# First pass of a decoder layer: the softplus of the state-space block summed by VectorE instead of by identity products in PSUM

## The chip, the core and the metric

The kernel runs on one core of one Trainium2 chip. The metric is the device time of one execution in microseconds (us). Times of single instructions below are in nanoseconds (ns) or us, as marked.

## What is computed

One decoder layer over 128 sequences of 128 positions and width 256. It has three parts, each with a residual and a layer norm: a selective state-space block (Mamba), a cross attention with FiLM and a long convolution, and a mixture FFN. The change touches only the first one, and there only the step size `dt`:

```
xz = einsum('bld,ed->ble', x, in_proj_w);  xc, z = split(xz)
xs = silu(conv1d(xc) + conv_b)
dt, B, C = split(einsum('bld,rd->blr', xs, x_proj_w), [64, 80])
dt = softplus(einsum('blr,dr->bld', dt, dt_proj_w) + dt_proj_b)      # 512 channels
...
h[t] = exp(dt*A) * h[t-1] + dt*B*xs;   y[t] = sum over 16 states of h[t]*C[t]
```

With v the argument of the softplus, e = exp(-|v|) and w = -(1+e) rounded, the kernel computes softplus(v) as relu(v) + ln(-w) + r, where r = e + (w + 1) is what the rounding of w lost. So each element of `dt` is a sum of three terms.

## The kernel before, in words

The program has a setup and three passes over the data, with a barrier of all engines between them. Pass 1 (`pass1`) holds the state-space block, the first half of the cross attention (scores, top-k, softmax, FiLM) and ends at about 5.1 ms of the profile. It works on 32 blocks of 4 sequences (512 columns). The 512 channels are 4 chunks `c` of 128 partitions; each chunk has 16 states; so a block has 64 **units** `u`, one scan each.

For one unit: ScalarE makes the decay exp(dt*A) (`decay`, L1049). VectorE scans (`tensor_tensor_scan`, L1180 for odd units, L1184 for even ones). GpSimd multiplies the scanned state by C four units later (`times_c`, L1255), and TensorE adds it up over the states by an identity product in PSUM (`sum_states`, L877). The input of the scan is dt*B*xs: for even units GpSimd makes it (L1268), for odd units ScalarE scales the transposed product (L1036) and TensorE transposes it (L862). The scanned states lie in a ring of 8 tiles, so GpSimd's L1268 of unit u waits for TensorE's sum of unit u-8.

There is no scheduler. Every engine runs its own list in order, and all meet by semaphores (`need`). While block i is scanned, the steps of the **front** of block i+1 and of the **back** of block i-1 are put between the units by hand: the tables `PE_AT`, `ACT_AT`, `DVE_AT` and `POOL_AT` say after which unit a step is issued on each engine. The steps that matter here:

- `dt0` to `dt3` (ScalarE, after units 31 to 38): |v| into `small` (L952) and relu(v) into `dt` (L954).
- `se` (ScalarE, 39): e = exp(-|v|) in `small` (L959), then w into `uu` (L962).
- `sr` (VectorE, 38): r into `small` (L1111), over all four chunks at once.
- `sl` (ScalarE, 40): ln(-w) in `uu` (L965), with a load of the table of Ln before it and one of Exp behind it.
- `ds0` to `ds3`: TensorE (42, 43, 44, 51) adds r, ln and relu of one chunk in PSUM by three products with the identity (L775, L777, L779), and ScalarE (44, 46, 48, 52) copies the sum into `dt` (L968).
- `sp0` to `sp3` (GpSimd, 45, 48, 53, 59): dt*xs (L1247), which waits for `dt` of its chunk. GpSimd's products of later units are queued behind it.
- `tka` to `tkd` and `sm` with a number (VectorE): top-k and softmax of the back of the block before; each `tk` is four MAX8 and four MATCH_REPLACE8 (L1137, L1141), `sm` is L1152 and L1158. `sc2`, `sc3` (L824, L825) and `at2` (L833) are score and attention products on TensorE, and `sm2` on ScalarE (L995) is the exponential that VectorE's `sm2` waits for.

`PER` has the counts of the semaphores for one block, and `BANK` gives the tiles of the steps two PSUM banks in turn.

Of the kernel before, what the change touches and what calls it, by code (L numbers as in the profile page):

```python
# [78 lines left out]
    ld_C0=128, ld_C1=128, ld_C2=128, ld_C3=128, bt_mm=1, bt=1, ut_mm=4, ut=4,  # L79
    vabs=4, vrelu=4, vexp=1, w1=1, rest=1, vln=1, ds_mm=4, dt=4, u=4,  # L80
    decay=64, bx=32, bxt=32, bxp=32, scan=64, hc=64, nsum=64, y=4, yg=4,
# [12 lines left out]
PE_AT = dict(xc0=2, xc1=3, xc2=6, xc3=7, op0=8, op1=8, op2=9, op3=10, z0=13, z1=13, z2=14, x1T=17, z3=19, qk=21,  # L94
             sc0=22, xp=24, bt=26, dt0=29, sc1=29, dt1=30, dt2=34, at0=35, dt3=36, sc2=36, at1=40, ds0=42, ds1=43,
             ds2=44, sc3=45, at2=49, ds3=51, tu0=53, at3=53, xa=54, tu1=55, film0=56, film1=58, tu2=59, film2=60,
             tu3=60, film3=62)
ACT_AT = dict(xc0=5, y3=5, xc1=5, xc2=6, xc3=9, z0=12, x1=14, z1=14, z2=15, x1T=16, z3=19, qk=23, si=24, xp=26,
              sm0=26, bt=28, dt0=31, dg0=31, dt1=33, dt2=34, sm1=36, dt3=38, at0=39, se=39, dg1=39, sl=40, at1=42,
              sm2=44, ds0=44, ds1=46, dg2=46, ds2=48, at2=49, sm3=50, ds3=52, dg3=52, at3=53, tu0=53, xa=54, tu1=56,  # L100
              tu2=62, tu3=63)
DVE_AT = dict(xc0=4, xc1=4, xc2=5, xc3=6, ln1=12, ln2=18, tka0=24, tkb0=24, tkc0=24, tkd0=26, sm0=26, tka1=31,
              tkb1=32, tkc1=33, tkd1=34, sm1=35, tka2=38, sr=38, tkb2=39, tkc2=40, tkd2=41, sm2=42, tka3=46, tkb3=47,
              tkc3=48, tkd3=49, sm3=49, film0=57, film1=59, film2=62, film3=63)
# [3 lines left out]
def steps_at(table, u, which):  # L108
# [8 lines left out]
    dt0=("vrelu", 1), dt1=("vrelu", 2), dt2=("vrelu", 3), dt3=("vrelu", 4),  # L117
    ds0=("dt", 1), ds1=("dt", 2), ds2=("dt", 3), ds3=("dt", 4),
    tu0=("ut", 1), tu1=("ut", 2), tu2=("ut", 3), tu3=("ut", 4),
# [369 lines left out]
def pass1(nc, sems, i_, arena, psum, x1_d, xa_d, xin_d, wf_d, bc_d, kr_d, sh, NB):  # L489
    with ExitStack() as ctx:  # L490
# [72 lines left out]
        def tile_ps(name):  # L563
            return side[:, BANK[name]]
# [148 lines left out]
        def _(pe):  # L713
# [14 lines left out]
            def step(name, i, par, other, which):  # L728
# [33 lines left out]
                elif name[:2] == "tu":  # L762
# [6 lines left out]
                    mm.then_inc(S["ut_mm"], 1)  # L769
                elif name[:2] == "ds":  # L770

                    c = int(name[-1])
                    ps = bank(name)
                    need(pe, "rest", i, 1)
                    pe.matmul(ps, ident, small[:, c], start=True, stop=False)  # L775
                    need(pe, "vln", i, 1)
                    pe.matmul(ps, ident, uu[par][:, c], start=False, stop=False)  # L777
                    need(pe, "vrelu", i, c + 1)
                    pe.matmul(ps, ident, dt[par][:, c], start=False, stop=True).then_inc(S["ds_mm"], 1)  # L779
                elif name[:2] == "op":  # L780
# [133 lines left out]
        def _(act):  # L914
            def step(name, i, par):
# [29 lines left out]
                elif name[:2] == "dt":  # L945
                    need(act, "dt_mm", i, c + 1)
                    if c == 0:
                        need(act, "ds_mm", i - 1, C)
                        need(act, "st_xin", i - 3, 64)
                        need(act, "q_mm", i - 2, 1)  # L950
                        need(act, "u", i - 2, C)
# [11 lines left out]
                elif name == "sl":  # L963
                    need(act, "rest", i, 1)
                    act.activation(uu[par], uu[par], ACT.Ln, scale=-1.0).then_inc(S["vln"], 1)  # L965
                elif name[:2] == "ds":
                    need(act, "ds_mm", i, c + 1)
                    act.copy(dt[par][:, c], tile_ps(name)).then_inc(S["dt"], 1)  # L968
                elif name == "x1":
# [117 lines left out]
        def _(dve):  # L1087
# [8 lines left out]
            def step(name, i, par):  # L1096
# [11 lines left out]
                elif name == "sr":  # L1108

                    need(dve, "w1", i, 1)  # L1110
                    dve.scalar_tensor_tensor(out=small, in0=uu[par], scalar=1.0, in1=small, op0=ALU.add, op1=ALU.add)\  # L1111
                       .then_inc(S["rest"], 1)
                elif name == "ln1":
                    need(dve, "ld_x", i, 16)
# [56 lines left out]
            def iteration(i, par, front, back):  # L1171
                names = which_steps(front, back)
                for u in range(C * NS):
                    need(dve, "decay", i, u + 1)
                    s = ring[:, u % RING]
                    if through_pe(u):
                        need(dve, "bxp", i, u // 2 + 1)
                        j, w = before(i, u, RING)
                        need(dve, "nsum", j, w + 1)
                        dve.tensor_tensor_scan(s, decay_sb[:, u // 2 % 2], bx_ps[:, u // 2 % 2], 0.0, ALU.mult, ALU.add)\  # L1180
                            .then_inc(S["scan"], 1)
                    else:
                        need(dve, "bx", i, u // 2 + 1)
                        dve.tensor_tensor_scan(s, decay_ps[:, u // 2 % 2], s, 0.0, ALU.mult, ALU.add)\  # L1184
                            .then_inc(S["scan"], 1)
                    for st in steps_at(DVE_AT, u, names):
                        if st == "film0" and front:
                            need(dve, "ds_mm", i + 1, C)
                        if st in FRONT:
                            step(st, i + 1, 1 - par)  # L1190
                        else:
                            step(st, i - 1, 1 - par)
# [748 lines left out]
```

## Time and profile before

| | |
|---|---|
| median of 3 runs | 7288.89 us (7283.7 to 7292.69) |
| the profiled execution | 7288.94 us, its span 7287.1 us |
| granted clock of TensorE, mean | 0.955 |
| busy share of the span: TensorE, VectorE, ScalarE, GpSimd | 92%, 74%, 61%, 63% |

The profile is of one execution. An instruction's row has its start, its length, its engine, its line in the program, its tiles (`arena` is all of SBUF, `psum` all of PSUM), and in brackets how long the engine sat idle before it and what ended the wait. Matmuls are pipelined: a row of two or four products of 512 columns is longer than the distance from one start to the next, and float32 products show two records each.

### The profile page before, as it was taken

To read this page: it belongs to the slowest core of one execution; us is meant where nothing else is said; L and a number is where in the kernel's file an instruction comes from. 1 tells how busy PE (TensorE), PEld (TensorE's weight loads), DVE (VectorE), ACT (ScalarE), POOL (GpSimd) and SP (SyncE) were. 2 spreads that over 40 slices of the span, in tenths; PEclk is the share of its full clock that TensorE was granted. 3 is DMA by queue.
4 is the path that set the end of the run, shared out by engine and by line. 5 is a ranking of instruction groups with operands and counts; after the bars stand their busy time and mean duration, and the time that the engine had idled before them with its cause. 6 is when DMAs were issued, how large, how long until landed. Compare 5 with 4: busy or idle time off the path is not lost. (4 is left out here: it accounts for less than half of the span.)

```text
span 7287.1 us, 107870 instructions
## 1 busy us (share of the span) xinstructions
PE 6717.7 (92%) x25168; PEld 3749.4 (51%) x25168; DVE 5404.4 (74%) x13962; ACT 4452.2 (61%) x9788; POOL 4596.0 (63%) x3991
## 2 busy tenths in 40 slices
PE   3899999999999999999999999997789999999997
PEld 1354455554555444454445554554656666666664
DVE  5588888888888888888888888886336666666665
ACT  2788888788887888878888788885212212221111
POOL 0788888888888888888888888897011111111111
PEclk6999999999999999999999999998789999999998
DMA  1556556665566656656556565555611111111110
GB/s 41 137 146 150 137 143 157 148 151 142 143 154 154 145 142 142 148 153 149 143 137 152 157 149 145 139 154 170 204 36 35 32 32 32 32 32 32 32 32 20
DMA packets 554213, 835.19 MB, mean 115 GB/s; under 512 B 169179, under 2 KB 207388, under 8 KB 551712
## 3 DMA queue, kind: packets, MB, share of 16 engines
q1 hardware_dynamic: 552768, 820.23, 44.5%
q10 hardware_dynamic: 864, 8.65, 0.3%
q8 instruction: 189, 3.10, 0.2%
q14 instruction: 392, 3.21, 0.1%
HBM read 745.91 MB, written 74.45 MB: 113 GB/s over the span
## 5 line engine op out<-in xcount | busy, mean ns | idle before, releaser
L1255 POOL TENSOR_TENSOR arena<-arena 128x512 f32<-128x512 f32 x2048 | 2588.2, 1279 | 308.3 <-DVE arena L1180 258.6
L877 PE MATMUL psum<-arena 128*128 128x512 f32 x4096 | 2156.2, 622 | 30.0 <-POOL arena L1255 24.0
L1180 DVE TENSOR_TENSOR_SCAN arena<-arena,psum 128x512 f32<-128x512 f32 x1024 | 1236.4, 1207 | 379.5 <-ACT arena L1049 292.6
L1268 POOL TENSOR_TENSOR arena<-arena 128x512 f32<-128x512 f32 x1024 | 1334.5, 1303 | 121.8 <-PE psum L877 121.4
L1036 ACT ACTIVATE arena<-arena 128x128 f32<-128x128 f32 x4096 | 1301.8, 394 | 141.6 <-PE psum L862 141.0
L1184 DVE TENSOR_TENSOR_SCAN arena<-psum,arena 128x512 f32<-128x512 f32 x1024 | 1234.4, 1205 | 86.7 <-issue 38.7
L877 PEld LDWEIGHTS psum<-arena 128*128 128x128 f32 x4096 | 703.9, 197 | 570.0 <-issue 379.4
L1834 POOL TENSOR_SCALAR arena<-arena 128x4 f32<-128x4 f32 x160 | 36.8, 230 | 1164.9 <-DVE arena L1695 1164.9
L1049 ACT ACTIVATE arena<-arena 128x508 f32<-128x508 f32 x1024 | 735.9, 719 | 57.9 <-DVE arena L1180 57.1
L862 PEld LDWEIGHTS psum<-arena 128*128 128x128 f32 x4096 | 515.5, 146 | 492.9 <-issue 438.5
L1049 ACT ACTIVATE psum<-arena 128x508 f32<-128x508 f32 x1024 | 699.7, 683 | 50.5 <-DVE arena L1180 31.0
L862 PE MATMUL psum<-arena 128*128 128x128 f32 x4096 | 646.4, 282 | 41.1 <-issue 18.3
L1658 ACT ACTIVATE arena<-psum,arena 128x512 f32<-128x512 f32 x256 | 176.3, 689 | 621.7 <-PE psum L1565 621.7
L740 PE MATMUL psum<-arena 128*128 128x512 f32 x1024 | 479.9, 597 | 30.6 <-ACT arena L1073 28.1
L1565 PE MATMUL psum<-arena 128*128 128x512 f32 x1024 | 449.8, 597 | 1.4 <-ACT arena L1652 1.4
L1576 PE MATMUL psum<-arena 128*128 128x256 f32 x2048 | 447.2, 379 | 0.0
L1576 PEld LDWEIGHTS psum<-arena 128*128 128x128 f32 x2048 | 389.0, 190 | 66.7 <-issue 15.4
L1141 DVE MATCH_REPLACE8 arena<-arena 128x128 f32<-128x128 f32 x1536 | 407.0, 278 | 0.0
L1104 DVE SCALAR_TENSOR_TENSOR arena<-psum,arena 128x508 f32<-128x508 f32 (+2 forms) x384 | 282.7, 743 | 122.7 <-ACT arena L921 113.7
L1843 POOL TENSOR_TENSOR arena<-arena 128x1024 f32<-128x1024 f32 x32 | 75.2, 2351 | 448.2 <-DVE arena L1733 448.2
L740 PEld LDWEIGHTS psum<-arena 128*128 128x128 f32 x1024 | 195.7, 192 | 278.9 <-issue 267.1
L1137 DVE MAX8 arena<-arena 128x8 f32<-128x128 f32 x1536 | 327.3, 275 | 7.6
(218 smaller groups left out, 10304.8 us busy)
## 6 DMA issues: line engine op xcount, KB each, us to landing
arena<-bc_scratch SPq DMA_DIRECT2D x1152, 512.0 KB, 5.2
arena<-in_xT_dram SPq DMA_DIRECT2D x32, 512.0 KB
arena<-in_x_dram SPq DMA_DIRECT2D x32, 512.0 KB, 7.7
x_scratch<-arena SPq DMA_DIRECT2D x32, 512.0 KB, 5.6
xin_scratch<-arena SPq DMA_DIRECT2D x128, 128.0 KB, 2.5
arena<-kernel_scratch SPq DMA_DIRECT2D x32, 512.0 KB, 6.4
arena<-x_scratch SPq DMA_DIRECT2D x32, 512.0 KB, 3.7
out_dram<-arena SPq DMA_DIRECT2D x32, 512.0 KB
```

The lines of the kernel that those rows point to most:

```text
L740: mm = pe.matmul(ps, win[:, k, e0:e0 + P], xT[:, k], start=k == 0, stop=k == DH - 1)
L862: mm = pe.transpose(bx_ps[:, v % 2, b * L:(b + 1) * L], bxt[:, v % 2, b * P:(b + 1) * P], ident)
L877: pe.matmul(y_ps, ident, ring[:, u % RING], start=False, stop=n == NS - 1).then_inc(S["nsum"], 1)
L1036: a = act.activation(bxt[:, v % 2, b * P:(b + 1) * P], uT(par, c)[:, b * P:(b + 1) * P], ACT.Identity, scale=BT[par][:, b, state(u):state( ...
L1049: act.activation(seqs(decay)[:, :, 1:L], seqs(dt[par][:, c])[:, :, 1:L], ACT.Exp, scale=negA[:, c, k:k + 1]).then_inc(S["decay"], 1)
L1141: a = dve.match_replace(left[:, h], v8[:, r, h], src[:, h], NEG)
L1180: dve.tensor_tensor_scan(s, decay_sb[:, u // 2 % 2], bx_ps[:, u // 2 % 2], 0.0, ALU.mult, ALU.add)\
L1184: dve.tensor_tensor_scan(s, decay_ps[:, u // 2 % 2], s, 0.0, ALU.mult, ALU.add)\
L1255: pool.tensor_tensor(h, h, Cb[:, u // 2 % PAIRS, u % 2], ALU.mult).then_inc(S["hc"], 1)
L1268: pool.tensor_tensor(ring[:, u % RING], uu[par][:, c], Bb[:, state(u)], ALU.mult)\
L1565: mm = pe.matmul(psum[:, m % 2], w1[:, k, m * P:(m + 1) * P], hT[:, k], start=k == 0, stop=k == DH - 1)
L1576: mm = pe.matmul(psum[:, 2 + o, bb * D:(bb + 1) * D], gT[:, m, b * L:(b + 1) * L], w2[:, m], start=m == 0, stop=m == 7)
```

## The change

The 12 products with the identity (per block) and the four copies are gone. VectorE's step `sr` gets a second instruction: dt = dt + small over all four chunks (128x2048), behind waits for relu of all chunks and for its own result r. New steps `ds0` to `ds3` on VectorE, after units 43, 43, 44 and 45, add `uu` (ln) to one chunk of `dt` each (128x512). GpSimd waits for the same semaphore `dt` as before. The guard before `film0`, which writes into the memory of `small`, now waits for the first sum. The order of the three terms in the sum is another one.

```diff
-DVE_AT = dict(... tkd2=41, sm2=42, tka3=46, ...)
+DVE_AT = dict(... tkd2=41, sm2=42, ds0=43, ds1=43, ds2=44, ds3=45, tka3=46, ...)
...
-                elif name[:2] == "ds":
-
-                    c = int(name[-1])
-                    ps = bank(name)
-                    need(pe, "rest", i, 1)
-                    pe.matmul(ps, ident, small[:, c], start=True, stop=False)
-                    need(pe, "vln", i, 1)
-                    pe.matmul(ps, ident, uu[par][:, c], start=False, stop=False)
-                    need(pe, "vrelu", i, c + 1)
-                    pe.matmul(ps, ident, dt[par][:, c], start=False, stop=True).then_inc(S["ds_mm"], 1)
...
                 elif name[:2] == "dt":
                     need(act, "dt_mm", i, c + 1)
                     if c == 0:
-                        need(act, "ds_mm", i - 1, C)
+                        need(act, "dt", i - 1, C)
...
-                elif name[:2] == "ds":
-                    need(act, "ds_mm", i, c + 1)
-                    act.copy(dt[par][:, c], tile_ps(name)).then_inc(S["dt"], 1)
...
                     dve.scalar_tensor_tensor(out=small, in0=uu[par], scalar=1.0, in1=small, op0=ALU.add, op1=ALU.add)\
                        .then_inc(S["rest"], 1)
+                    need(dve, "vrelu", i, C)
+                    need(dve, "rest", i, 1)
+                    dve.tensor_tensor(dt[par], dt[par], small, ALU.add).then_inc(S["vsum"], 1)
+                elif name[:2] == "ds":
+                    need(dve, "vln", i, 1)
+                    need(dve, "vsum", i, 1)
+                    dve.tensor_tensor(dt[par][:, c], dt[par][:, c], uu[par][:, c], ALU.add).then_inc(S["dt"], 1)
...
                         if st == "film0" and front:
-                            need(dve, "ds_mm", i + 1, C)
+                            need(dve, "vsum", i + 1, 1)
```

The order of VectorE's instructions around unit 38, in a block of the loop, before the change (the scan of unit 38 stands just ahead of the first row; the last rows are the scan of unit 39 and the start of `tkb2`; in the program's own list a scan is named SCALAR_TENSOR_TENSOR):

```order
L1137 MAX arena<-psum 128x8 x4
L579 REGISTER_ALU
L1141 MATCH_REPLACE arena<-arena,psum 128x128 x4
L573 REGISTER_ALU
L1111 SCALAR_TENSOR_TENSOR arena<-arena 128x2048
L573 REGISTER_ALU
L1180 SCALAR_TENSOR_TENSOR arena<-arena,psum 128x512
```

and the same place in the changed kernel, whose line numbers are some lower:

```order
L1129 MAX arena<-psum 128x8 x4
L577 REGISTER_ALU
L1133 MATCH_REPLACE arena<-arena,psum 128x128 x4
L571 REGISTER_ALU
L1096 SCALAR_TENSOR_TENSOR arena<-arena 128x2048
L1100 TENSOR_TENSOR arena<-arena 128x2048
L571 REGISTER_ALU
L1172 SCALAR_TENSOR_TENSOR arena<-arena,psum 128x512
```

One sum of 2048 columns now stands between r and the scan of unit 39. The second place is VectorE from `sm2` (unit 42) to the scan of unit 46, before:

```order
L1152 SCALAR_TENSOR_TENSOR arena<-arena,psum 128x128 x4
L1158 RECIPROCAL arena<-arena 128x4
L573 REGISTER_ALU
L1180 SCALAR_TENSOR_TENSOR arena<-arena,psum 128x512
L573 REGISTER_ALU x2
L1184 SCALAR_TENSOR_TENSOR arena<-psum,arena 128x512
L573 REGISTER_ALU
L1180 SCALAR_TENSOR_TENSOR arena<-arena,psum 128x512
L573 REGISTER_ALU x2
L1184 SCALAR_TENSOR_TENSOR arena<-psum,arena 128x512
```

and changed:

```order
L1144 SCALAR_TENSOR_TENSOR arena<-arena,psum 128x128 x4
L1150 RECIPROCAL arena<-arena 128x4
L571 REGISTER_ALU
L1172 SCALAR_TENSOR_TENSOR arena<-arena,psum 128x512
L1104 TENSOR_TENSOR arena<-arena 128x512 x2
L571 REGISTER_ALU x2
L1176 SCALAR_TENSOR_TENSOR arena<-psum,arena 128x512
L1104 TENSOR_TENSOR arena<-arena 128x512
L571 REGISTER_ALU
L1172 SCALAR_TENSOR_TENSOR arena<-arena,psum 128x512
L1104 TENSOR_TENSOR arena<-arena 128x512
L571 REGISTER_ALU x2
```

Two sums stand behind the scan of unit 43, and one each behind those of units 44 and 45. Each of the five new instructions reads two tiles of SBUF and writes one.

## Rows read from the trace of the kernel before

**Rows 1.** The page, part 1: busy time, share of the span and instructions by engine.
```profile
PE 6717.7 (92%) x25168; PEld 3749.4 (51%) x25168; DVE 5404.4 (74%) x13962; ACT 4452.2 (61%) x9788; POOL 4596.0 (63%) x3991
```

**Rows 2.** Busy time in one millisecond of pass 1; the columns are named in its first line.
```profile
core 0: us, PE busy (x) PEld busy (x) DVE busy (x) ACT busy (x) POOL busy (x), PEclk, DMA share, GB/s
3000.00:4000.00 1000.00, 953.89 (x3373) 495.88 (x3372) 841.00 (x2228) 821.48 (x1884) 864.36 (x727) 0.97 0.58 145
```

**Rows 3.** VectorE's L1111 in blocks 6 to 26: ns min/median/max, first and last start.
```profile
L1111 DVE SCALAR_TENSOR_TENSOR arena<-arena x21: 2293/2294/2568, 1053.4 to 4103.6; 128x2048 f32<-128x2048 f32 x21
```

**Rows 4.** GpSimd's waits from 2000 to 3000 us: in total, times, longest.
```profile
POOL arena L1255 <- DVE arena L1180: 51.2, 35, 2.4
...
POOL arena L1247 <- ACT arena L968: 21.6, 6, 3.6
```

**Rows 5.** Instructions in order of time, VectorE, block 14, units 38 to 46.
```profile
2422.64 2.56 DVE L1111 SCALAR_TENSOR_TENSOR arena<-arena 128x2048 f32<-128x2048 f32 x1 [1.52 <-ACT arena L962]
2425.12 1.21 DVE L1180 TENSOR_TENSOR_SCAN arena<-arena,psum 128x512 f32<-128x512 f32 x1
...
2434.51 1.21 DVE L1184 TENSOR_TENSOR_SCAN arena<-psum,arena 128x512 f32<-128x512 f32 x1
2436.73 0.29 DVE L1152 SCALAR_TENSOR_TENSOR arena<-arena,psum 128x128 f32<-128x128 f32 x1 [1.01 <-ACT psum L995]
...
2437.88 1.22 DVE L1180 TENSOR_TENSOR_SCAN arena<-arena,psum 128x512 f32<-128x512 f32 x1
2439.02 1.20 DVE L1184 TENSOR_TENSOR_SCAN arena<-psum,arena 128x512 f32<-128x512 f32 x1
```

**Rows 6.** The same stretch on ScalarE: `sl`, and the copy of `ds0`.
```profile
2427.19 1.91 ACT L965 ACTIVATE arena<-arena 128x2048 f32<-128x2048 f32 x1
...
2436.60 0.61 ACT L968 COPY arena<-psum 128x512 f32<-128x512 f32 x1
```

**Rows 7.** The same stretch on GpSimd.
```profile
2421.77 1.27 POOL L1268 TENSOR_TENSOR arena<-arena 128x512 f32<-128x512 f32 x1 [2.16 <-PE psum L877]
2423.01 4.67 POOL L1255 TENSOR_TENSOR arena<-arena 128x512 f32<-128x512 f32 x2
...
2432.67 1.28 POOL L1255 TENSOR_TENSOR arena<-arena 128x512 f32<-128x512 f32 x1 [1.79 <-DVE arena L1180]
2437.37 1.09 POOL L1247 TENSOR_TENSOR arena<-arena 128x512 f32<-128x512 f32 x1 [3.42 <-ACT arena L968]
2438.42 1.27 POOL L1268 TENSOR_TENSOR arena<-arena 128x512 f32<-128x512 f32 x1
2439.65 2.49 POOL L1255 TENSOR_TENSOR arena<-arena 128x512 f32<-128x512 f32 x2
```

**Rows 8.** Busy time in block 14 from `sp0` on, columns as in rows 2.
```profile
2437.40:2485.90 48.50, 47.59 (x184) 25.78 (x185) 42.39 (x96) 39.20 (x100) 48.47 (x40) 1.00 0.73 157
```

**Rows 9.** Instructions in order of time, TensorE, block 14: `ds3`, and where it meets GpSimd.
```profile
2451.58 1.02 PE L775 MATMUL psum<-arena 128*128 128x512 f32 x2
...
2454.15 0.60 PE L862 MATMUL psum<-arena 128*128 128x128 f32 x4
...
2458.14 1.13 PE L833 MATMUL psum<-arena 128*128 128x128 f32 x8 [0.38 <-ACT arena L1008]
2459.11 0.60 PE L862 MATMUL psum<-arena 128*128 128x128 f32 x4
2459.55 1.02 PE L877 MATMUL psum<-arena 128*128 128x512 f32 x2
```

**Rows 10.** The same view of GpSimd, the C product that this sum waits for.
```profile
2457.70 2.51 POOL L1255 TENSOR_TENSOR arena<-arena 128x512 f32<-128x512 f32 x2
```

**Rows 11.** Single lines over the span, as in rows 3: a sum of 1024 columns (pass 3), GpSimd's L1268.
```profile
L1752 DVE TENSOR_TENSOR arena<-arena x32: 1226/1227/1229, 5382.4 to 7236.2; 128x1024 f32<-128x1024 f32 x32
...
L1268 POOL TENSOR_TENSOR arena<-arena x1024: 1252/1274/3308, 209.3 to 5049.0; 128x512 f32<-128x512 f32 x171
```

**Rows 12.** TensorE waits, and its granted clock shortly after (columns as in rows 2).
```profile
2415.46 0.23 PE L824 MATMUL psum<-arena 1*128 1x128 bf16 x1 [2.32 <-DVE arena L1152]
...
2417.70:2421.00 3.30, 3.30 (x7) 1.78 (x8) 3.20 (x14) 3.19 (x5) 1.91 (x2) 0.50 0.74 151
```

**Rows 13.** The first block, ahead of the loop: L965 and the first L775 and L1247.
```profile
192.99 1.91 ACT L965 ACTIVATE arena<-arena 128x2048 f32<-128x2048 f32 x1 [1.06 <-DVE arena L1111]
193.10 2.04 PE L775 MATMUL psum<-arena 128*128 128x512 f32 x2 [8.94 <-DVE arena L1111]
...
199.59 1.09 POOL L1247 TENSOR_TENSOR arena<-arena 128x512 f32<-128x512 f32 x1 [65.47 <-ACT arena L968]
```

More of the change, by code:

```diff
@@ L79 @@
     ld_C0=128, ld_C1=128, ld_C2=128, ld_C3=128, bt_mm=1, bt=1, ut_mm=4, ut=4,
-    vabs=4, vrelu=4, vexp=1, w1=1, rest=1, vln=1, ds_mm=4, dt=4, u=4,
+    vabs=4, vrelu=4, vexp=1, w1=1, rest=1, vsum=1, vln=1, dt=4, u=4,
     decay=64, bx=32, bxt=32, bxp=32, scan=64, hc=64, nsum=64, y=4, yg=4,
@@ L94 @@
 PE_AT = dict(xc0=2, xc1=3, xc2=6, xc3=7, op0=8, op1=8, op2=9, op3=10, z0=13, z1=13, z2=14, x1T=17, z3=19, qk=21,
-             sc0=22, xp=24, bt=26, dt0=29, sc1=29, dt1=30, dt2=34, at0=35, dt3=36, sc2=36, at1=40, ds0=42, ds1=43,
-             ds2=44, sc3=45, at2=49, ds3=51, tu0=53, at3=53, xa=54, tu1=55, film0=56, film1=58, tu2=59, film2=60,
+             sc0=22, xp=24, bt=26, dt0=29, sc1=29, dt1=30, dt2=34, at0=35, dt3=36, sc2=36, at1=40, sc3=45, at2=49, tu0=53, at3=53, xa=54, tu1=55, film0=56, film1=58, tu2=59, film2=60,
              tu3=60, film3=62)
@@ L99 @@
               sm0=26, bt=28, dt0=31, dg0=31, dt1=33, dt2=34, sm1=36, dt3=38, at0=39, se=39, dg1=39, sl=40, at1=42,
-              sm2=44, ds0=44, ds1=46, dg2=46, ds2=48, at2=49, sm3=50, ds3=52, dg3=52, at3=53, tu0=53, xa=54, tu1=56,
+              sm2=44, dg2=46, at2=49, sm3=50, dg3=52, at3=53, tu0=53, xa=54, tu1=56,
               tu2=62, tu3=63)
 DVE_AT = dict(xc0=4, xc1=4, xc2=5, xc3=6, ln1=12, ln2=18, tka0=24, tkb0=24, tkc0=24, tkd0=26, sm0=26, tka1=31,
-              tkb1=32, tkc1=33, tkd1=34, sm1=35, tka2=38, sr=38, tkb2=39, tkc2=40, tkd2=41, sm2=42, tka3=46, tkb3=47,
+              tkb1=32, tkc1=33, tkd1=34, sm1=35, tka2=38, sr=38, tkb2=39, tkc2=40, tkd2=41, sm2=42, ds0=43, ds1=43, ds2=44, ds3=45, tka3=46, tkb3=47,
               tkc3=48, tkd3=49, sm3=49, film0=57, film1=59, film2=62, film3=63)
@@ L117 @@
     dt0=("vrelu", 1), dt1=("vrelu", 2), dt2=("vrelu", 3), dt3=("vrelu", 4),
-    ds0=("dt", 1), ds1=("dt", 2), ds2=("dt", 3), ds3=("dt", 4),
     tu0=("ut", 1), tu1=("ut", 2), tu2=("ut", 3), tu3=("ut", 4),
```

## The prediction

> **What bounds the kernel now.** I began with the shares of busy time. Over the span TensorE leads with 92% [rows 1], and in a millisecond of pass 1 it is busy for 954 us against 864 of GpSimd, 841 of VectorE and 821 of ScalarE [rows 2]. Read alone, this says that TensorE is the bound and that taking products from it must pay. But four engines above 80% that run fixed lists can each be the bound in a different part of a block, and the page's chain of waits covers only the last pass, so pass 1 must be read by its units. A block repeats every (4103.6 - 1053.4) / 20 = 152.5 us [rows 3].
>
> Next I read who waits for whom. GpSimd waits for the very thing that the change makes: L1247 (`sp0`) waits for the copy of `ds0`, 21.6 us in 6 blocks, 3.6 us each [rows 4]. In order of time, block 14 shows it: `sp0` starts at 2437.37 after 3.42 us idle [rows 7], just behind ScalarE's copy, which ends at 2436.60 + 0.61 = 2437.21 [rows 6]. From there to 2485.9 GpSimd is busy for 48.47 of 48.50 us [rows 8]. So **when `sp0` starts decides when the next 48 us of GpSimd's list are done**; there is no slack in it. TensorE is nearly full in the same stretch (47.59 us), but behind GpSimd: it does its sum of the unit at 2459.55 [rows 9], 0.6 us after GpSimd finished that product at about 2458.95 (half of the 2.51 us behind 2457.70) [rows 10], and only from then on has it a backlog of its own.
>
> VectorE is the third party. From its L1111 to the scan of unit 43 it has one wait, 1.01 us ahead of `sm2` [rows 5]. GpSimd's C products wait for its scans [rows 4, 7]. Hence what is put on VectorE between units 38 and 45 comes almost undiluted.
>
> **What is removed.** Twelve products per block on TensorE. Three of one chunk take 2454.15 - 2451.58 = 2.57 us [rows 9], so 10.3 us per block. The first nine stand where GpSimd is waiting or TensorE keeps up with it; they hold up nothing that GpSimd needs within 8 units. `ds3` lies just ahead of the place where TensorE and GpSimd meet; with it gone TensorE follows GpSimd closer there, and I credit 0.5 us of the 0.6. ScalarE loses four copies of 0.6 us, one of them the one that `sp0` waited for; its exponential for `sm2` ends before that copy and comes no earlier.
>
> **What is added, per block** (block 14's clock).
> 1. The sum of 2048 columns behind L1111. L1111 has the same size and two SBUF inputs: 2.29 us [rows 3]. It delays the scan of unit 39 (2425.12).
> 2. Contention with GpSimd. L1268 takes 1.27 us in the median, 3.31 at most [rows 11]. In block 14 L1111 was issued 0.4 us before the end of an L1268, took 2.56 instead of 2.29 us [rows 5], and the next two GpSimd products took 4.67 us together where two take 2.5 (2.49 at 2439.65) [rows 7]. So an instruction of VectorE with two inputs in SBUF and a product of GpSimd do not run together: the later one stands still. The Trainium skill has this as a rule (SBUF — State Buffer, the section on ports: a DVE instruction with two SBUF inputs contends with a GpSimd instruction that reads SBUF, the second to issue fully blocks); the trace agrees, with these 2.2 us. The new sum finds the blocked product of GpSimd in front of it and waits for its rest, 0 to 1.27 us; I take 0.6. Delay of unit 39: 2.9 us.
> 3. Up to unit 42 nothing gives it back; ahead of `sm2` the 1.0 us of waiting do. Unit 43's scan ends at 2439.02 + 0.07 + 1.9 = 2441.0 instead of 2439.1.
> 4. `ds0` adds 0.69 us: L1752 takes 1.23 us for 1024 columns and L1111 2.29 for 2048 [rows 3, 11], so 0.53 us per 512 and 0.16 fixed. With the release of 0.16 us (2437.37 - 2437.21) `sp0` starts at 2441.9: **4.5 us later**. ScalarE's Ln ended at 2429.1 [rows 6] and is no part of it.
> 5. `ds1`, `ds2`, `ds3` fall into GpSimd's stretch without slack, and each stops it for its 0.6 us: 1.9 us.
> 6. Less the 0.5 us from above: 4.5 + 1.9 - 0.5 = **+5.9 us per block**.
>
> Block i+1's front is made while block i is scanned, so this comes 31 times: 183 us. The first front runs alone: Ln ends at 194.9, `sp0` starts at 199.59 [rows 13]; now the first sum runs beside Ln and `ds0` ends about 196.0, 3.5 us earlier. Sum: +183 - 3.5 = +179 us on 7288.94, the profiled execution's time, which is also the median to 0.1 us: **7468 us**. The delay is late for all engines alike: the next block's first products of the front stand in TensorE's list behind its sums, which wait for GpSimd.
>
> **Bounds.** Without any contention: 2.3 - 1.0 + 2.6 = 3.9 for `sp0`, nothing in 5, so +3.4 per block, 7391 us. With the full wait in 2, and 2.0 in 5, and no credit: 5.1 + 2.0 = 7.1 per block, 7506 us. I take the middle, nearest to block 14, since it shows the contention at this very place.
>
> **Rivals.**
> - *No contention of the new sums* (they may slip between products of GpSimd): 7391 us. For it: most L1268 show 1.27 us; against: those beside L1111 do not. Chance 0.14.
> - *TensorE's clock falls as well.* After 2.32 us of waiting it ran at half clock (0.50, that is 1.2 GHz) a little later [rows 12]. With `ds` gone and GpSimd late, TensorE has about 4 us of nothing between `sc3` and the sum of unit 42. At half clock its sums take 1.7 us against GpSimd's 1.3 to 2.5 per unit; `at2` and with it ScalarE's exponential come some 1.6 us later still: 31 x 1.6 = 50, 7518 us. Chance 0.10.
> - *Faster.* If VectorE could add `ds0` before 2437.2, GpSimd's wait of 3.6 us would vanish: -31 x 3.6 = -112, 7177 us; or, if TensorE's backlog and not GpSimd's decides, `ds3` comes back: -31 x 2.57 = -80, 7209 us. The point that decides is the scan of unit 43, behind which `ds0` stands: it ends at 2439.1 even before anything is added, 1.9 us too late. The Trainium skill speaks for this side (Perfetto Trace Analysis, Identifying the Most-Contended Engine: optimize first the engine with the highest occupancy); the same section warns that TensorE's headroom is not read from its matmul occupancy. Its rule would have the 10.3 us count. Chance 0.14.
> - *No difference*, 7289 us: the slip is taken back where GpSimd waits for scans (1.79 us in rows 7, and others) since TensorE has 10 us less to do. It needs a block whose start does not hang on GpSimd's last product. Chance 0.06.
> - That the edit does not do what it says is excluded: the lists of both engines show it.
>
> **Numbers.** The forecast, 7468, has 0.56. The range takes in both bounds and most of the clock case: 7345 to 7520. About 0.2% (15 us) is what a measurement tells from no change. Faster 0.14, within it 0.06, slower 0.80.
>
> **What would show it.** `sp0` should wait some 5 us (3.4 before), now for VectorE's sum; the distance of two L1111 should be 158 us; GpSimd products beside the five sums should show 1.9 us and more where 1.27 is usual, and the sums themselves more than 2.29 and 0.69. TensorE's busy time should fall by some 230 us (31 times most of 10.3, less what waits hide) without any gain. A period of 152.5 or less, or `sp0` without a wait, would prove me wrong.

## The result, and the profile after

| | before | changed |
|---|---|---|
| median of 4 runs each, us | 7290.79 (7283.7 to 7310.83) | 7455.19 (7433.85 to 7464.37) |
| ratio | | 1.0224, 95% interval 1.0204 to 1.0244 |
| profiled execution: time, span, us | 7288.94, 7287.1 | 7433.85, 7432.0 |
| mean granted clock of TensorE | 0.955 | 0.93 |

The change is slower by 2.2%, 164 us by the medians. The profiled execution is the fastest of its four runs and shows 145 us of it.

The page, part 1, busy time of each engine, as in [rows 1]:

```profile
PE 6557.6 (88%) x24400; PEld 3646.7 (49%) x24400; DVE 5607.4 (75%) x14122; ACT 4396.7 (59%) x9660; POOL 4698.4 (63%) x3991
```

The windows view of the same millisecond as in [rows 2]:

```profile
core 0: us, PE busy (x) PEld busy (x) DVE busy (x) ACT busy (x) POOL busy (x), PEclk, DMA share, GB/s
3000.00:4000.00 1000.00, 900.56 (x3129) 469.29 (x3128) 846.12 (x2065) 770.93 (x1763) 860.83 (x712) 0.93 0.60 145
```

TensorE is busy for 160 us less over the span and 53 us less in the millisecond, and the program is longer. GpSimd has the same 3991 instructions as before and is busy for 102 us more: the same products, made slower.

The single lines of VectorE and GpSimd that the change made or moved (ns min/median/max, first and last start; the first row in blocks 6 to 26 as in [rows 3], the others over the span):

```profile
L1096 DVE SCALAR_TENSOR_TENSOR arena<-arena x21: 2293/2294/2566, 1066.8 to 4221.3; 128x2048 f32<-128x2048 f32 x21
...
L1100 DVE TENSOR_TENSOR arena<-arena x32: 2292/3173/3179, 191.2 to 5008.8; 128x2048 f32<-128x2048 f32 x32
L1104 DVE TENSOR_TENSOR arena<-arena x128: 658/682/1681, 193.6 to 5029.6; 128x512 f32<-128x512 f32 x128
L1239 POOL TENSOR_TENSOR arena<-arena x128: 1080/1100/1536, 194.6 to 5056.8; 128x512 f32<-128x512 f32 x128
```

L1096 is the old L1111: a block repeats every (4221.3 - 1066.8) / 20 = 157.7 us, 5.2 more than before [rows 3]. The first sum (L1100) is a shorter operation than its median of 3.17 us: alone it takes 2.29.

GpSimd's waits from 2000 to 3000 us, against [rows 4] (L1239 is the old L1247, L1247 the old L1255, L1260 the old L1268):

```profile
POOL arena L1247 <- DVE arena L1172: 52.6, 33, 2.4
POOL arena L1239 <- DVE arena L1104: 33.5, 7, 4.8
POOL arena L1260 <- PE psum L865: 24.2, 7, 3.9
```

`sp0` now waits 33.5 / 7 = 4.8 us per block, for VectorE's sum and no longer for ScalarE's copy (3.6 before).

Block 14 on VectorE in order of time, against [rows 5]:

```profile
2485.32 2.29 DVE L1096 SCALAR_TENSOR_TENSOR arena<-arena 128x2048 f32<-128x2048 f32 x1 [0.83 <-ACT arena L950]
2487.72 3.17 DVE L1100 TENSOR_TENSOR arena<-arena 128x2048 f32<-128x2048 f32 x1
2490.81 1.21 DVE L1172 TENSOR_TENSOR_SCAN arena<-arena,psum 128x512 f32<-128x512 f32 x1
...
2501.34 0.26 DVE L1144 SCALAR_TENSOR_TENSOR arena<-arena,psum 128x128 f32<-128x128 f32 x1
...
2502.46 1.22 DVE L1172 TENSOR_TENSOR_SCAN arena<-arena,psum 128x512 f32<-128x512 f32 x1
2503.60 1.27 DVE L1104 TENSOR_TENSOR arena<-arena 128x512 f32<-128x512 f32 x2
2504.79 1.21 DVE L1176 TENSOR_TENSOR_SCAN arena<-psum,arena 128x512 f32<-128x512 f32 x1
2505.92 1.68 DVE L1104 TENSOR_TENSOR arena<-arena 128x512 f32<-128x512 f32 x1
2507.52 1.21 DVE L1172 TENSOR_TENSOR_SCAN arena<-arena,psum 128x512 f32<-128x512 f32 x1
2508.65 0.66 DVE L1104 TENSOR_TENSOR arena<-arena 128x512 f32<-128x512 f32 x1
```

and on GpSimd, against [rows 7]:

```profile
2485.98 2.76 POOL L1260 TENSOR_TENSOR arena<-arena 128x512 f32<-128x512 f32 x1 [2.98 <-PE psum L865]
2488.70 4.67 POOL L1247 TENSOR_TENSOR arena<-arena 128x512 f32<-128x512 f32 x2
...
2504.43 1.39 POOL L1239 TENSOR_TENSOR arena<-arena 128x512 f32<-128x512 f32 x1 [4.78 <-DVE arena L1104]
2505.78 1.27 POOL L1260 TENSOR_TENSOR arena<-arena 128x512 f32<-128x512 f32 x1
2507.01 3.42 POOL L1247 TENSOR_TENSOR arena<-arena 128x512 f32<-128x512 f32 x2
```

Read them together. L1260, issued at 2485.98 beside L1096, stands until L1096 ends at 2487.61 and is done at 2488.74: 2.76 us where it takes 1.27 alone. The sum begins at 2487.72 and stands for the rest of L1260, so that it takes 3.17 us for 2.29, and then the two products behind L1260 take 4.67 us where two take 2.5. Further on `sp0` starts 0.83 us after the start of the first `ds` sum, the one that it waits for.

The windows view from `sp0` on (columns as above), against [rows 8], and two short stretches in it:

```profile
2504.40:2553.00 48.60, 44.76 (x163) 24.01 (x163) 42.44 (x93) 34.77 (x88) 48.58 (x40) 0.90 0.73 152
2505.00:2508.40 3.40, 2.24 (x9) 1.32 (x8) 3.40 (x3) 2.20 (x6) 3.40 (x3) 0.50 0.00 0
2508.40:2512.00 3.60, 3.22 (x4) 1.23 (x5) 3.50 (x13) 0.94 (x2) 3.60 (x4) 0.50 0.13 13
```

GpSimd is again without a gap (48.58 of 48.60 us). TensorE is now loose beside it, 44.76 us busy although it ran at half clock (0.50) for a part of the time.

The first block, ahead of the loop, in order of time on ScalarE, against [rows 13]:

```profile
191.16 1.91 ACT L953 ACTIVATE arena<-arena 128x2048 f32<-128x2048 f32 x1 [1.06 <-DVE arena L1096]
```

and on GpSimd, where `sp0` is the first of the four:

```profile
194.57 5.35 POOL L1239 TENSOR_TENSOR arena<-arena 128x512 f32<-128x512 f32 x4 [61.01 <-DVE arena L1104]
```

### The profile page after: what moved, and what is told of

The parts are those of the page before. It is cut to its first block and busy times, and to the rows that moved or that the text cites. A ratio compares the mean times of both kernels' runs of the same rounds, so it can differ in the third digit from the quotient of the medians.

```text
span 7432.0 us, 106398 instructions
## 1 busy us (share of the span) xinstructions
PE 6557.6 (88%) x24400; PEld 3646.7 (49%) x24400; DVE 5607.4 (75%) x14122; ACT 4396.7 (59%) x9660; POOL 4698.4 (63%) x3991
## 5 line engine op out<-in xcount | busy, mean ns | idle before, releaser
L1247 POOL TENSOR_TENSOR arena<-arena 128x512 f32<-128x512 f32 x2048 | 2671.0, 1318 | 345.5 <-DVE arena L1172 279.5
L865 PE MATMUL psum<-arena 128*128 128x512 f32 x4096 | 2274.0, 654 | 160.0 <-POOL arena L1247 152.1
L1260 POOL TENSOR_TENSOR arena<-arena 128x512 f32<-128x512 f32 x1024 | 1337.4, 1306 | 108.7 <-PE psum L865 108.6
L865 PEld LDWEIGHTS psum<-arena 128*128 128x128 f32 x4096 | 727.7, 205 | 781.7 <-POOL arena L1247 433.7
L850 PEld LDWEIGHTS psum<-arena 128*128 128x128 f32 x4096 | 523.6, 150 | 697.8 <-issue 436.5
L850 PE MATMUL psum<-arena 128*128 128x128 f32 x4096 | 674.4, 290 | 201.8 <-DVE arena L1172 177.6
L738 PE MATMUL psum<-arena 128*128 128x512 f32 x1024 | 479.4, 596 | 30.4 <-ACT arena L1058 27.6
L1557 PE MATMUL psum<-arena 128*128 128x512 f32 x1024 | 449.3, 596 | 1.4 <-ACT arena L1644 1.4
L1568 PEld LDWEIGHTS psum<-arena 128*128 128x128 f32 x2048 | 389.0, 190 | 66.7 <-issue 15.4
L738 PEld LDWEIGHTS psum<-arena 128*128 128x128 f32 x1024 | 195.5, 191 | 277.9 <-issue 267.5
```

Source lines behind the costliest of these rows:

```text
L738: mm = pe.matmul(ps, win[:, k, e0:e0 + P], xT[:, k], start=k == 0, stop=k == DH - 1)
L850: mm = pe.transpose(bx_ps[:, v % 2, b * L:(b + 1) * L], bxt[:, v % 2, b * P:(b + 1) * P], ident)
L865: pe.matmul(y_ps, ident, ring[:, u % RING], start=False, stop=n == NS - 1).then_inc(S["nsum"], 1)
L1247: pool.tensor_tensor(h, h, Cb[:, u // 2 % PAIRS, u % 2], ALU.mult).then_inc(S["hc"], 1)
L1260: pool.tensor_tensor(ring[:, u % RING], uu[par][:, c], Bb[:, state(u)], ALU.mult)\
L1557: mm = pe.matmul(psum[:, m % 2], w1[:, k, m * P:(m + 1) * P], hT[:, k], start=k == 0, stop=k == DH - 1)
```

## Experiments

Each time below is a median, with the lowest and the highest run; a ratio is to the kernel before, run on the same chip. The chips differ between experiments, so two of them are best compared by their ratios; 0.1% is 7.3 us. The first four tell what each part of the change costs.

### 1. No sum at all

From the changed kernel; `dt` stays relu of the input, r and the logarithm are not added.

```diff
-                    dve.tensor_tensor(dt[par], dt[par], small, ALU.add).then_inc(S["vsum"], 1)
-                elif name[:2] == "ds":
-                    need(dve, "vln", i, 1)
-                    need(dve, "vsum", i, 1)
-                    dve.tensor_tensor(dt[par][:, c], dt[par][:, c], uu[par][:, c], ALU.add).then_inc(S["dt"], 1)
...
-                    need(pool, "dt", i, c + 1)
+                    need(pool, "vln", i, 1)
```

> The changed kernel without any of the five sums: dt is relu(v) alone, r and the logarithm are computed and not added; L1247 (sp0) waits for the logarithm. My theory (the start of sp0 sets the next 48 us of GpSimd's list): its wait of 3.6 us vanishes, 31 x 3.6 = 112 less than before, about 7180 us. Rival 1, TensorE's throughput decides: 10.3 us per block less, 6970 us. Rival 2, another chain of equal length stands behind sp0: 7289, no change against before.

Measured: 7253.94 us (7247.35 to 7255.06), ratio 0.9954 [0.9937, 0.997]: only 31 us faster than before, 1.0 per block, with the sums, the products and the copies all gone. GpSimd in block 14:

```profile
2408.59 1.28 POOL L1240 TENSOR_TENSOR arena<-arena 128x512 f32<-128x512 f32 x1 [1.78 <-DVE arena L1165]
2409.81 1.10 POOL L1232 TENSOR_TENSOR arena<-arena 128x512 f32<-128x512 f32 x1
2410.86 1.27 POOL L1253 TENSOR_TENSOR arena<-arena 128x512 f32<-128x512 f32 x1
2412.09 1.27 POOL L1240 TENSOR_TENSOR arena<-arena 128x512 f32<-128x512 f32 x1
2415.11 1.27 POOL L1240 TENSOR_TENSOR arena<-arena 128x512 f32<-128x512 f32 x1 [1.75 <-DVE arena L1165]
```

and the scan that it waits for, on VectorE:

```profile
2413.81 1.22 DVE L1165 TENSOR_TENSOR_SCAN arena<-arena,psum 128x512 f32<-128x512 f32 x1
```

`sp0` (L1232 here) starts with no wait, as an edit that makes `ds0` cheap enough would have it. Three products later GpSimd stands for the scan of unit 43. The expectation (7180 us) failed: a second limit lies close behind the first, and taking away `sp0`'s wait of 3.4 us, with the products and the copies, was worth 1.0. Experiments 6 and 8 ask for the wait alone.

### 2. The same sums with one input

From the changed kernel; each of the five sums becomes a maximum over the same tile, of nearly the same duration, with one input in SBUF. r and the logarithm are not added here either.

```diff
-                    dve.tensor_tensor(dt[par], dt[par], small, ALU.add).then_inc(S["vsum"], 1)
+                    dve.tensor_reduce(spare[:, C:C + 1], dt[par].rearrange("p c t -> p (c t)"), AX.X, ALU.max).then_inc(S["vsum"], 1)
...
-                    dve.tensor_tensor(dt[par][:, c], dt[par][:, c], uu[par][:, c], ALU.add).then_inc(S["dt"], 1)
+                    dve.tensor_reduce(spare[:, c:c + 1], dt[par][:, c], AX.X, ALU.max).then_inc(S["dt"], 1)
```

> The changed kernel with each of the five sums replaced by a maximum over the same tile of dt (one SBUF input, one column out, no tile rewritten), so dt stays relu(v). If contention with GpSimd is part of the cost: the trace of the change shows 0.9 us of waiting in the first sum and 1.2 us lost by GpSimd after sp0, 2.1 us per block, 65 us in all, so about 7390 us. If VectorE's own time is all of it: 7455, like the change.

Measured: 7378.16 us (7364.05 to 7380.63), ratio 1.0123 [1.0106, 1.014]. The lines over the span:

```profile
L1101 DVE TENSOR_REDUCE arena<-arena x32: 2285/2286/2287, 192.1 to 4951.6; 128x1 f32<-128x2048 f32 x32
L1105 DVE TENSOR_REDUCE arena<-arena x128: 657/662/686, 194.5 to 4970.5; 128x1 f32<-128x512 f32 x128
```

None of the 32 long ones is over 2.287 us, where the sum has a median of 3.173. The ratios differ by 1.0224 - 1.0123 = 1.0%: about 75 of the 164 us are contention (55 to 95 by the two intervals), the rest is VectorE's plain time. A maximum differs from a sum in a second point, it writes no tile. That this is not what counts is seen on VectorE's scans in the changed kernel, which read one tile in SBUF, the other in PSUM, and write a whole one to SBUF:

```profile
L1172 DVE TENSOR_TENSOR_SCAN arena<-arena,psum x1024: 1186/1209/1222, 207.5 to 5206.5; 128x512 f32<-128x512 f32 x171
```

None of the 1024 is over 1.222 us, with GpSimd busy for 86% of the time beside them.

### 3. The first sum alone

From the kernel before; r is added by VectorE, two products per chunk stay.

```diff
-                    need(pe, "rest", i, 1)
-                    pe.matmul(ps, ident, small[:, c], start=True, stop=False)
                     need(pe, "vln", i, 1)
-                    pe.matmul(ps, ident, uu[par][:, c], start=False, stop=False)
-                    need(pe, "vrelu", i, c + 1)
+                    pe.matmul(ps, ident, uu[par][:, c], start=True, stop=False)
+                    need(pe, "vsum", i, 1)
...
+                    dve.tensor_tensor(dt[par], dt[par], small, ALU.add).then_inc(S["vsum"], 1)
```

> The kernel before with the first sum alone on VectorE (relu + r, 2048 columns), and two products with the identity and the copy per chunk left. My theory: VectorE comes 3.1 us late to unit 39 and 2 us late to unit 43, but sp0 still waits for ScalarE's copy at the same time and the next products of GpSimd need units 42 and 43 only 2 us later: 7289 to 7310 us. Rival, every us put on VectorE before unit 45 counts: 31 x 2.0 = 62, 7350 us.

Measured: 7324.02 us (7303.11 to 7333.13), ratio 1.0043 [1.0026, 1.0059], 39 us by the medians, between the two expectations. GpSimd's waits, 2000 to 3000 us:

```profile
POOL arena L1256 <- DVE arena L1181: 56.1, 40, 3.4
...
POOL arena L1248 <- ACT arena L966: 2.7, 7, 0.4
```

`sp0`'s wait for the copy is nearly gone (2.7 us in 7, before 21.6 in 6 [rows 4]): the 3 us by which VectorE is late now reach GpSimd as a longer wait for a scan (3.4, before 2.4), and are for the most part taken from the wait at `sp0`. In block 14 `sp0` starts 14.7 us after the start of r, as before. With ScalarE's copy as the last to come, the first sum is cheap.

### 4. The chunk sums alone

From the changed kernel, without the first sum; r is left out of `dt`.

```diff
-                    dve.tensor_tensor(dt[par], dt[par], small, ALU.add).then_inc(S["vsum"], 1)
...
-                    need(dve, "vsum", i, 1)
+                    need(dve, "vrelu", i, C)
```

> The changed kernel without the first sum (r is computed and left out of dt), ds0 to ds3 on VectorE as in the change. My theory: unit 43's scan ends at the time of before, 1.9 us after sp0 used to start, ds0 adds 0.8: sp0 2.5 us later than before; contention 1.2, less 0.5 of TensorE: +3.2 us per block, 7388 us. Rival, the parts add up from VectorE's time alone (2.8 of 5.1 us): +2.9 per block, 7378; rival, contention is nothing: +2.0, 7351.

Measured: 7373.18 us (7363.62 to 7378.02), ratio 1.012 [1.0104, 1.0137], 88 us or 2.9 per block. This is nearer to the rival by VectorE's time alone (2.9) than to the theory (3.2), and it cannot tell the two apart; experiment 2 does. The two parts alone make 39 + 88 = 127 us, and together 164. In 3 the lateness of the scan of unit 43 hides behind ScalarE's copy. Here `sp0` follows that scan, which is on time, and starts 17.2 us after the start of r in block 14, 2.5 later than before (14.7). With both parts it follows a scan that is 1.9 late, nothing hides that any more, and it starts 4.4 later.

### 5. TensorE's work given back

From the changed kernel; at the places of the old `ds` steps TensorE makes three products per chunk again, of a weight tile, which nobody reads.

```diff
+                elif name[:2] == "ds":
+                    c = int(name[-1])
+                    ps = bank(name)
+                    need(pe, "vln", i, 1)
+                    for k in range(3):
+                        mm = pe.matmul(ps, ident, win[:, 0, 0:T], start=k == 0, stop=k == 2)
+                    mm.then_inc(S["ds_mm"], 1)
```

> The changed kernel with TensorE's twelve products per block put back at their old places, now of a tile of weights and read by nobody. If the removed products were worth nothing and TensorE's clock costs nothing: 7455 us, the change's time. If the products were on the path behind ds3: +0.5 to +2.6 us per block, 7470 to 7535. If the change's time has 1.6 us per block of TensorE at half clock, which the products would keep up: 7405.

Measured: 7464.42 us (7449.23 to 7471.19), ratio 1.025 [1.0236, 1.0264]; the change has 1.0224 [1.0204, 1.0244]. The windows view (columns as above):

```profile
3000.00:4000.00 1000.00, 944.56 (x3266) 493.02 (x3265) 843.75 (x2104) 766.72 (x1761) 864.52 (x711) 0.94 0.57 142
```

TensorE is busy for 44 us more in the millisecond, and the time is 9 us longer by the medians, 0.26% or 19 us by the ratios, whose intervals overlap. **The products that the change takes from TensorE, the engine with the largest busy share, are 31 x 10.3 = 319 us of its work and buy 9 to 19 us of time, hardly more than the noise.** TensorE's mean granted clock is 0.943 here against 0.93 in the change. This run gives back the products and a part of the clock together, so it shows what the two are worth in sum and not each by itself.

### 6 and 8. The kernel before, with `sp0` released earlier

These touch no sum. ScalarE copies `ds0` at unit 42 (6), and makes the exponential of `sm2` at 43 as well (8).

```diff
-              sm2=44, ds0=44, ds1=46, ...
+              ds0=42, sm2=44, ds1=46, ...
```
```diff
-              sm2=44, ds0=44, ds1=46, ...
+              ds0=42, sm2=43, ds1=46, ...
```

> The kernel before with ScalarE's copy of ds0 two units earlier (42 instead of 44), nothing else. The kernel without sums showed that GpSimd, freed of sp0's wait of 3.4 us, runs 1.5 us further and then waits for VectorE's scan of unit 43. So: about 1.0 us per block, 31 in all, 7258 us. If the wait of sp0 were the bound by itself: 7180. If ScalarE's other work, now 0.6 us later, counts as much: 7289.

> As e6, and ScalarE's exponential sm2 one unit earlier (43 instead of 44), so that VectorE doesn't wait 1.0 us for it ahead of unit 43. If the scan of unit 43 is the second limit behind sp0: up to another 1.0 us per block, 7227 us. If not: like e6.

Measured: 7284.08 us (7270.5 to 7298.0, 11 runs), ratio 1.0006 [0.9996, 1.0015], and 7285.58 us (7274.72 to 7293.24, 11 runs), ratio 1.0011 [1.0002, 1.002]. GpSimd's waits in 6, 2000 to 3000 us, beside [rows 4]:

```profile
POOL arena L1255 <- DVE arena L1180: 64.9, 41, 2.4
```

The row for `sp0` is gone, all 21.6 us of it, and the waits for the scans rise from 51.2 to 64.9 us. The time does not move; the expected gain of 1.0 us per block is not there. With the computation whole, `sp0`'s wait is worth nothing.

In 8 the scan of unit 43 comes earlier as well, and GpSimd waits 0.65 us for it, where it waits 1.75 in experiment 1. The time does not move either. One step on, VectorE's `tka3` (unit 46) stands for the scores of `sc3`, the L825 behind L824 on TensorE:

```profile
2440.74 1.27 POOL L1255 TENSOR_TENSOR arena<-arena 128x512 f32<-128x512 f32 x1 [0.65 <-DVE arena L1180]
...
2446.22 0.89 DVE L1137 MAX8 arena<-psum 128x8 f32<-128x128 f32 x4 [2.23 <-issue]
...
2440.41 1.02 PE L775 MATMUL psum<-arena 128*128 128x512 f32 x2
...
2443.94 0.22 PE L824 MATMUL psum<-arena 1*128 1x128 bf16 x1
```

The profile names no releaser for this wait, but the last L825 ends at 2446.12, just before. TensorE has no gap to speak of from 2436.44 on, and six of the products with the identity (`ds1`, `ds2`) stand in its list ahead of `sc3`. That wait of `tka3` was 0.74 us before the change, and in experiment 1, without the products, there is none. So the scan of unit 43 is not the whole of the second limit: with `sp0` early, TensorE's products come onto the path. That this is why 1 gains 31 us and 6 and 8 gain nothing is likely, and no run shows it.

### 7. One chunk at a time

From the changed kernel; both sums of a chunk as two instructions of 512 columns, placed just ahead of each `sp`, at units 41, 47, 51 and 56.

```diff
-... tkd2=41, sm2=42, ds0=43, ds1=43, ds2=44, ds3=45, tka3=46, tkb3=47,
-... sm3=49, film0=57, ...
+... tkd2=41, ds0=41, sm2=42, tka3=46, ds1=47, tkb3=47,
+... sm3=49, ds2=51, ds3=56, film0=57, ...
```

> The sums of the change by chunk, two of 512 columns each, at units 41, 47, 51 and 56 in place of 38 and 43 to 45. sp0 then starts with unit 41, some 7 us earlier than in the change, VectorE is 1.3 us late to unit 42 and on time at 43. My theory: what is left is contention, at most 8 x 0.6 us less what falls into GpSimd's waits, and 1.3 us of VectorE at unit 47: +1.0 to +3.0 us per block on before, 7320 to 7380 us. Rival, VectorE's busy time as such counts (5.1 us per block, wherever it stands): 7450, like the change.

Measured: 7571.96 us (7569.4 to 7591.85, 5 runs), ratio 1.041 [1.0396, 1.0424], slower than the change by 117 us (medians) or 1.9% (ratios). The expectation failed. GpSimd's waits, 2000 to 3000 us:

```profile
POOL arena L1239 <- DVE arena L1104: 64.8, 24, 4.0
```

and VectorE in block 14:

```profile
2561.99 0.68 DVE L1101 TENSOR_TENSOR arena<-arena 128x512 f32<-128x512 f32 x1
2562.77 0.69 DVE L1104 TENSOR_TENSOR arena<-arena 128x512 f32<-128x512 f32 x1
```

24 waits in some six blocks: every `sp` waits, not the first alone. I had placed the sums by unit number, just ahead of the unit at which GpSimd wants each of them. But GpSimd's C products run four units behind: at its unit 48, where `sp1` stands, it needs the scan of unit 44 only, and VectorE reaches unit 47, and with it `ds1`, later than that. Besides, `ds0` came behind `tkd2`, which stands first at unit 41. These two sums show no contention (0.68 and 0.69), and the medians over the span are the same (0.679 and 0.692), so what failed was the place.

### 9 and 10. `ds0` first, then `ds3` last

From the changed kernel: `ds0` at 41 and ahead of `tkd2`, the others as they were (9), and `ds3` at 54 besides (10).

```diff
-... tkc2=40, tkd2=41, sm2=42, ds0=43, ds1=43, ds2=44, ds3=45, tka3=46, ...
+... tkc2=40, ds0=41, tkd2=41, sm2=42, ds1=43, ds2=44, ds3=45, tka3=46, ...
```
```diff
-... sm2=42, ds1=43, ds2=44, ds3=45, tka3=46, ... sm3=49, film0=57, ...
+... sm2=42, ds1=43, ds2=44, tka3=46, ... sm3=49, ds3=54, film0=57, ...
```

> The changed kernel with ds0 right behind the scan of unit 41, ahead of tkd2 and sm2 (it stood behind unit 43). sp0 can then start some 5 us earlier than in the change. If the start of sp0 alone decides: about 4.6 us per block less than the change, 7312 us. If VectorE's lateness is a second limit close behind (its scans of units 47 to 50 come as late as in the change, 4 us later than before): GpSimd gets ahead and then waits for these scans, 1 to 2 us per block less than the change, 7390 to 7425. If only VectorE's busy time counts: 7455.

> As e9, and ds3 behind unit 54 instead of 45, where VectorE has waits of 2.7 us in the change and sp3 comes 5 units later. With VectorE's lateness as the second limit: 0.7 us of VectorE and up to 0.6 us of contention less in the full stretch, 20 to 40 us below e9. If it makes sp3 wait, as the late sums did in the kernel with sums by chunk: e9's time or more.

Measured: 7396.99 us (7389.81 to 7401.89, 5 runs), ratio 1.0155 [1.0141, 1.0169], and 7369.63 us (7358.24 to 7376.95, 4 runs), ratio 1.0115 [1.0098, 1.0133]. GpSimd's waits in 9, 2000 to 3000 us:

```profile
POOL arena L1247 <- DVE arena L1172: 65.5, 43, 3.4
...
POOL arena L1247 <- DVE arena L1176: 20.9, 21, 3.0
```

and GpSimd in block 14 of it:

```profile
2485.28 1.10 POOL L1239 TENSOR_TENSOR arena<-arena 128x512 f32<-128x512 f32 x1
...
2489.69 1.64 POOL L1247 TENSOR_TENSOR arena<-arena 128x512 f32<-128x512 f32 x1 [0.86 <-DVE arena L1172]
```

`sp0` starts without a wait and all 4.8 us of it are gone; 1.6 to 1.9 us per block come back in time (50 us by the ratios, 58 by the medians), and the waits for scans rise from 52.6 + 12.2 to 65.5 + 20.9 us in the millisecond. Moving `ds3` past VectorE's full stretch brings 27 us more. Version 10 halves the loss, and it is still 1.2% slower than the kernel before. No version with the sums on VectorE beat it.

## Why the prediction was right, step by step

The forecast of +179 us stands against +164 (medians) and +145 (profiled execution). Per block it was 5.9 us, and 5.2 are measured. The path was right: the sums make VectorE late, `sp0` starts later by that, and GpSimd's full list passes it on. In block 14, each against the start of r (L1111, now L1096):

| step | predicted | measured |
|---|---|---|
| 1 + 2, scan of unit 39 later | +2.9 | 5.49 - 2.48 = +3.0 |
| 3, end of the scan of unit 43 | +1.9 | 18.36 - 16.46 = +1.9 |
| 4, start of `sp0` | +4.5 | 19.11 - 14.73 = +4.4 |

The third row reads: before 2437.37 - 2422.64, now 2504.43 - 2485.32. It is 2.5 above the row over it since `sp0` followed ScalarE's copy before, and ran ahead of the end of that scan by 1.7 us; now it comes 0.75 us behind it.

- **Step 2**, the wait of the first sum, was taken as 0.6 us and is 0.9 (3.17 against 2.29), with 0.3 gained back: L1096 itself is undisturbed in this block, and L1111 took 2.56. The bounds of 0 to 1.27 held. That this is contention with GpSimd is shown by experiment 2, where a maximum over the same tile is never disturbed. The Trainium skill's rule (SBUF — State Buffer, Who interferes with whom) speaks of two SBUF inputs on the DVE side. Experiment 2 and the scans agree with it, and its price here is about 75 of 164 us.
- **Step 3** came as written: the wait of 1.01 us ahead of `sm2` is gone.
- **Step 5** was too large: 1.9 us predicted for `ds1` to `ds3`. From the start of `sp0` to the end of the second C product behind it there were 2439.65 + 2.49 - 2437.37 = 4.8 us, and now 2507.01 + 3.42 - 2504.43 = 6.0, 1.2 more. Who arrives second waits, and that was VectorE once: the `ds2` sum took 1.68 us for 0.66.
- **Step 6**: 4.4 + 1.2 = 5.6, and the block is longer by 5.2, so the credit of 0.5 is about right by its sum. It is not shown to be TensorE's. Experiment 5 shows only that all twelve products together are worth 0.3 to 0.6 us per block (9 to 19 us), with an interval that reaches down to nothing.
- **The first front** was put at -3.5 us. `sp0` starts 199.59 - 194.57 = 5.0 us earlier. Of these 1.8 lie ahead of ScalarE's Ln, which itself begins earlier (191.16, before 192.99) and of which the step knew nothing; behind it there are 3.2. But the step priced `sp0` alone. The other three `sp` no longer wait for products and copies of their own either, and the first scan starts at 205.73, before at 215.05: 9.3 us earlier.

The profiled execution adds up so: from the first scan to the last one of pass 1 (5053.6, now 5206.5) it is 162 us longer, which is 31 x 5.2; less 9.3 of the first front, the last scan is 153 us late; 8 us come back behind it, 7 of them ahead of VectorE's first copy in pass 2, and no run tells their cause. This leaves 145. The forecast is thus 34 us above the execution that was read: 21 by the blocks (183 against 162), 6 by the first front and 8 by the end. That it lies only 15 above the medians is in part luck: the three other runs are 15 to 31 us slower than the profiled one. The prediction also calls its 5.9 the middle of its bounds; the middle of 3.4 and 7.1 is 5.3, nearer to what was measured.

TensorE's busy time fell by 160 us and not by 230. Two of its sums over the states (four records) take 3.79 us at the half clock at 2508.78, where two took 1.88 at the full clock before, so more time at half clock takes back a part; this I have not separated.

**The rivals.** *No contention* (7391) describes experiment 2, which takes the contention away and gives 7378, and not the change. *The clock falls too* (7518): its event happened, with granted clock 0.50 from 2505 to 2512, but not its price at that place, since GpSimd had no gap in that stretch (3.40 of 3.40 and 3.60 of 3.60 us busy). *No difference* is out. *Faster* was rightly given little, but its figures were wrong. It priced `sp0`'s whole wait (-112 us) and `ds3` (-80). Experiments 1, 6 and 8 took the first wait away and got -31, 0 and 0; experiment 5 puts all of TensorE's twelve products at 9 to 19 us. The Trainium skill says to optimize the engine with the highest occupancy first (Perfetto Trace Analysis, Identifying the Most-Contended Engine). Taken by TensorE's busy share of 92%, against which the section itself warns, this would have misled here.

So one statement of the prediction was wrong in one direction: that the start of `sp0` decides. It holds for lateness, which passes down GpSimd's full list undiluted. It does not hold for a gain: VectorE's scan of unit 43 ends 1.7 us behind it, and where that comes earlier too, in experiment 8, TensorE's scores for `tka3` are next. Which chain carries the whole block in experiment 1 I have not settled. Its 7254 us say only that without sums, products and copies a block is 1.0 us shorter, so that all of them together hold some 0.5% of the kernel before.

## What to carry to other kernels

When several engines run fixed lists at 80 to 95%, price an edit by where it lands in the list of the engine that is waited for: a delay passes on in full wherever the follower has no slack, and the removal of the same wait is worth at most the distance to the next limit (here 1.0 us and less for a wait of 3.4), so look for that one before you count it. Place work by the clock of the trace and not by the step number, as experiment 7 shows, and prefer, beside GpSimd, forms of VectorE's work with one input in SBUF.

## What the runs showed of the hardware

- Two float32 inputs from SBUF on VectorE against GpSimd's products: the sum of 2048 columns takes 2.29 us alone (the first block, where GpSimd waits) and 3.17 in the median beside GpSimd; a maximum over the same columns takes 2.285 to 2.287 at all times, and a scan with one input in SBUF and the other in PSUM 1.186 to 1.222. Of 32 sums the longest is 3.179.
- TensorE's mean granted clock in the millisecond fell from 0.97 to 0.93, with half clock from 2505 to 2512 us. GpSimd had no gap in these 7 us, so they cost nothing there; what the lower clock costs over a whole block no run separates.
